# A routed-expert kernel: four weight loads moved later, filler matmuls on TensorE, and two of four result tables read and added while the last experts run

## What is computed

```
x = x + attention(norm(x))      # 16 heads, 4 kv heads, causal, soft cap, rotary
x = x + ffn(norm(x))            # routed experts + shared expert
x = x + recurrence(norm(x))     # h = a*h + u over the 2048 tokens
x = x + ffn(norm(x))            # the same ffn weights again
# ffn: softmax of x @ gate.T over 64 experts, best 3 of 8 groups, best 6 experts of them
slot = flat * 96 + min(pos, 95)                 # 96 rows per expert
buf[slot] = x[tok]                              # (64*96, 256)
out = (silu(buf @ Wg.T) * (buf @ Wu.T)) @ Wd.T  # M = 176
y = sum over the 6 choices of out[slot] * weight;  return y + shared(x)
```

## Time and profile before

| what | us |
|---|---|
| median of 3 runs (lowest, highest) | 1233.53 (1233.43, 1235.91) |
| the profiled execution, its own time | 1236.23 |
| its span, first to last instruction | 1234.1 |
| TensorE busy | 997.5 |
| DVE busy | 520.1 |
| ACT busy | 739.3 |
| POOL busy | 410.5 |

### The profile page before, as it was taken

One profiled execution on the slowest core, in us unless ns is written; L12 is line 12 of the kernel. 1 busy time (PEld: TensorE's weight loads), 2 busy tenths in 40 slices (PEclk: granted clock), 3 DMA queues, 4 the chain that ended last, 5 costly groups with the idle time before them and its releaser, 6 DMA issues.

```text
span 1234.1 us, 20310 instructions
## 1 busy us (share of the span) xinstructions
PE 997.5 (81%) x7268; PEld 644.7 (52%) x7268; DVE 520.1 (42%) x1575; ACT 739.3 (60%) x982; POOL 410.5 (33%) x404
## 2 busy tenths in 40 slices
...
GB/s 352 394 392 78 1 1 1 18 2 11 49 50 23 18 33 90 2 21 4 142 264 234 292 289 290 109 151 271 50 121 109 160 66 125 268 290 279 268 63 330
DMA packets 94948, 176.21 MB, mean 143 GB/s; under 512 B 13134, under 2 KB 46895, under 8 KB 94848
## 3 DMA queue, kind: packets, MB, share of 16 engines
...
## 4 chain that ended last, share of the span: by engine, by line
PE 29%; POOL 11%; issue 4%; DMA 3%; DVE 3%; DVEq 1%; ACT 0%; POOLq 0%; SPq 0%; ACTq 0%
PE PS L1459 14%; PE PS L1470 9%; POOL expert_in L335 8%; POOL pause L343 3%; PE PS L1446 2%; PE PS L1515 1%; DMA XE<-expert_in 1%; PE PS L1499 1%; DMA spare_space<-expert_out 1%; DMA expert_in<-xp,didx 1%; PE PS L1548 1%; DMA expert_out<-ob,yidx 1%; PE PS L1389 0%; PE PS L1404 0%; POOL expert_out L1345 0%
## 5 line engine op out<-in xcount | busy, mean ns | idle before, releaser
L335 POOL DMA_INDIRECT expert_in<-xp,didx x192 | 193.6, 1008 | 618.2 <-ACT PR L779 496.6
L774 ACT ACTIVATE PR<-PS 128x1024 f32<-128x1024 f32 (+3 forms) x312 | 276.5, 960 | 30.8 <-PE PS L643 15.2
L779 ACT ACTIVATE PR<-PR 128x2048 f32<-128x2048 f32 (+3 forms) x156 | 274.1, 1759 | 0.0
L1345 POOL DMA_INDIRECT expert_out<-ob,yidx x128 | 180.6, 1411 | 157.4 <-ACT ob L1657 117.5
L663 PE MATMUL PS<-PR,V 128*32 128x512 f32 (+3 forms) x768 | 94.9, 568 | 43.4 <-ACT PR L779 43.4
L1906 DVE SCALAR_TENSOR_TENSOR gta<-gth,PS 88x192 f32<-88x192 f32 x128 | 44.8, 350 | 192.8 <-ACT gth L1647 192.8
L643 PE MATMUL PS<-QT,KT 96*128 96x512 bf16 (+3 forms) x384 | 103.7, 363 | 12.4 <-ACT PR L774 9.8
L1647 ACT ACTIVATE gth<-PS 88x192 f32<-88x192 f32 x128 | 41.8, 326 | 106.6 <-PE PS L1459 106.6
L1657 ACT ACTIVATE ob<-PS,wslot 96x256 f32<-96x256 f32 x128 | 60.1, 469 | 62.1 <-PE PS L1470 59.9
L1459 PEld LDWEIGHTS PS<-XT,spare_space 128*88 128x88 f32 x960 | 91.7, 163 | 8.8 <-issue 2.6
L668 PE MATMUL PS<-PR,V 128*32 128x256 f32 x960 | 66.8, 392 | 34.9 <-ACT PR L779 34.6
...
## 6 DMA issues: line engine op xcount, KB each, us to landing
...
spare_space<-expert_out SPq DMA_DIRECT2D x24, 512.0 KB, 6.2
...
```

The source lines that it names most:

```text
L335: pool.indirect_dma_start(out=buf_d[f], out_offset=bass.IndirectOffsetOnAxis(ap=didx[b][:, r, j:j + 1], axis=0), in_=xp[b][:, r, :], in_of ...
L774: act.activation(PR[:, n % 3, 2 * pr:2 * pr + 2, cols(v, s):CW], PS[:, S0 + 2 * pr:S0 + 2 * pr + 2, cols(v, s):CW], ACT.Tanh, scale=1.0 / ...
L779: act.activation(PR[:, n % 3, :, lo:CW], PR[:, n % 3, :, lo:CW], ACT.Exp, scale=SOFT_CAP).then_inc(exp_done, 1)
L1345: pool.indirect_dma_start(out=y_d[f], out_offset=bass.IndirectOffsetOnAxis(ap=yidx[:, n % 4, j:j + 1], axis=0), in_=ob[:, i % EU, :], in_o ...
```

## The change

It has five parts. Line numbers in it differ from those of the profile before.

1. **Late fetch (f = 0 only).** SP waits until the first `XE` load has landed before it issues the weights of places 10 to 13, and `wab` after them.
2. **Fillers.** `fill(n)` on TensorE issues n matmuls of the identity with 256 columns into a bank whose content nobody reads: 14 ahead of either `experts`, 12, 4 and 13 around the first overflow matmuls, 12, 8, 8 and then 2 at a time in the recurrence loop, 15 ahead of the last combination.
3. **Tables.** `table_of` gives experts 0 to 43 four tables as before, 44 to 55 three (0, 1, 2), and 56 to 63 two (0, 1). A send waits for the last send to the same table, which is now 4, then 3, then 2 experts back.
4. **Retired tables.** Table 3 is complete after expert 43, table 2 after expert 55. `retired_tables` on SP reads each in four pieces (chunks, 512 KB in runs of 1 KB) into `TA` and `TB`, which take the place of ring places whose experts are done; DVE adds the pieces of table 3 to X after experts 50, 52, 54 and 56, and those of table 2 after expert 63.
5. **At the end two tables are read** (`LATE = 2`), 2 KB per partition and tile in place of 4 KB, with one add less on DVE or two matmuls less on TensorE for each tile. `add_results(2)` moves behind `recur_inputs(0)`.

```diff
+LATE = 2
+TABLE_GROUPS = (0, 11, 12, 13, 14)
+def table_of(e):
+    return e % 4 if e < 44 else (e - 44) % 3 if e < 56 else e % 2
+def last_in_table(e, j):
+    return max([i for i in range(e) if table_of(i) == j], default=None)
...
+        TA, TB = (place_at(NACC * i, NACC).rearrange("p (i n) -> p i n", i=NT) for i in range(2))
+        GB = place_at(0, LATE).rearrange("p (r n) -> p r n", r=CT)
...
+            def retired_tables(f):
+                for j, space, used in ((3, TA, (46, 48, 50, 52)), (2, TB, (58, 59, 60, 61))):
+                    last = f * E + last_in_table(E, j)
+                    sp.wait_ge(y_sent[last % EU], 16 * (last // EU + 1))
+                    if j == 2:
+                        sp.wait_ge(tables_added, (2 * f + 1) * NC)
+                    for c in range(NC):
+                        sp.wait_ge(down_psum, f * E + used[c])
+                        rows = y_d[f][NACC * CW * c:NACC * CW * (c + 1), :]
+                        sp.dma_start(space[:, CT * c:CT * (c + 1), :], rows.rearrange("(i p k) c -> p i k c", p=P, k=NACC)[:, :, j, :])\
+                          .then_inc(table_ld[c], 16)
...
             first_spare(0)
+            sp.wait_ge(x_ld[0], 16)
+            first_spare2(0)
             sp.dma_start(wab[:], wab_d).then_inc(wab_loaded, 16)
-            first_spare2(0)
             experts(0)
+            retired_tables(0)
...
-                if e >= NACC:
-                    pool.wait_ge(y_sent[(i - NACC) % EU], 16 * ((i - NACC) // EU + 1))
+                if last_in_table(e, table_of(e)) is not None:
+                    last = f * E + last_in_table(e, table_of(e))
+                    pool.wait_ge(y_sent[last % EU], 16 * (last // EU + 1))
...
+            def fill(n, bank=V0):
+                for _ in range(n):
+                    pe.matmul(PS[:, bank, 0:2 * P], const("ident"), consts[:, 0:2 * P], start=True, stop=True, skip_group_check=True)
...
+                pe.wait_ge(out_copied, 2 * E)
+                fill(15)
                 pe.wait_ge(o95_loaded, 32)
-                pe.wait_ge(out_copied, 2 * E)
...
+            fill(14)
             experts(0)
+            pe.wait_ge(out_copied, E)
+            fill(12)
             overflow_rows(0)
+            fill(4)
             overflow_rows(1)
+            fill(13)
             turn_recur(0)
             for c in range(NC + 1):
                 k = NC + c - 1
                 if c:
+                    fill(8 if c == 1 else 2)
                     turn_rows(k)
                     logits(k)
                 if c < NC:
                     gates(c)
+                if c == 0:
+                    fill(12)
...
                 if c < NC:
+                    fill(8 if c == 0 else 2)
                     turn_state(c)
...
+            def add_table(f, j, space, c):
+                dve.wait_ge(table_ld[c], 16 * (2 * f + j + 1))
+                xc = X[:, CT * c:CT * (c + 1), :]
+                dve.tensor_tensor(xc, xc, space[:, CT * c:CT * (c + 1), :], ALU.add).then_inc(tables_added, 1)
...
+                    if e in (50, 52, 54, 56):
+                        add_table(f, 0, TA, (e - 50) // 2)
+                for c in range(NC):
+                    add_table(f, 1, TB, c)
...
-            add_results(2)
             for c in range(NC + 1):
...
                 if c < NC:
                     recur_inputs(c)
+                if c == 0:
+                    add_results(2)
```

41 lines of the change are left out of this document (19 added, 22 removed).

## The result

The changed kernel takes **1262.49 us** (median of 4 runs, 1255.8 to 1266.1); the kernel before, run beside it, 1234.72 us (median of 4, 1233.43 to 1236.26). The ratio is 1.0222 with a 95% interval of 1.0187 to 1.0256: slower by 28 us. I had said 1229.0 and 1211 to 1240, so both the number and the direction were wrong. The profiled execution of the changed kernel took 1264.41 us, its span is 1262.6.

What follows compares the result with a forecast made beforehand. TensorE was taken to bound the expert stages, transfers and a relay of engines the joints between. Terms -6.0 + 19 + 3 - 8.5 - 12 = -4.5 us gave 1231.7 profiled, 1229.0 us on the median's scale; range 1211 to 1240.

Steps and rivals of the forecast that it cites:

- The reads of table 3: Both expert stages: DVE waits behind expert 50 for a piece queued behind weights, then the clock is low; +19 us.
- Sends closer together: Last experts of both stages: sends on fewer tables wait for landings, delaying the last send; +3 us, bounds 0 and 15.
- two tables pace the last experts: Rival, from expert 56: landings at 6.6 us pace the sends, 15 us in place of 3, total 1241; chance 0.18.
- The end: After the last send: fewer bytes read and TensorE kept fast by 15 fillers; -12 us, bounds -5 and -13.
- the fillers do not hold the clock: Rival, at the end: the clock drops before O95 lands, giving 5 us in place of 12, total 1236; chance 0.12.
- Reading back in f = 0: Between the stages: fewer adds and bytes, and fillers, bring POOL's first dispatch earlier; -8.5 us, bounds -5 and -11.
- Late fetch: Start of the f = 0 experts: holding weights and wab back lets the first input land sooner; -6.0 us.
- Fillers ahead of the experts: Start of both stages: 14 fillers end 5 and 7 us before the inputs, so stages start at 1.2 GHz; nothing.
- The pieces of table 3 are in time: Rival, behind expert 50: the pieces arrive without a DVE wait, the 19 us fall away, total 1210; chance 0.17.

Runs made afterwards that it cites:

- experiment 3: Kernel before with only the change's tables and send waits (four, three, then two), all four tables read at the end, no late fetch or fillers: 1236.12 us.
- experiment 8: experiment 1 with only table 3 retired, three tables used and read to the end, 22 fillers behind the last expert: 1226.88 us.
- experiment 9: experiment 6 with DVE's adds of table 2 held until every send has landed and O95 read first: 1228.14 us.
- experiment 6: experiment 1 with 32 fillers in place of 15 behind the last expert: 1232.1 us.
- experiment 4: Kernel before with the late fetch and all fillers of the change, its four tables left as they were: 1231.26 us.
- experiment 7: experiment 1 without the 12 fillers ahead of chunk 2's overflow matmuls and with 17 in place of 8 ahead of the first transposes of rows: 1236.55 us.
- experiment 12: Kernel retiring table 3 alone, with the middle's fillers as in experiment 7, and 34 and 43 in place of 14 fillers ahead of the experts: 1223.34 us.
- experiment 1: Changed kernel with DVE adding table 3's pieces behind experts 56 to 59 in place of 50, 52, 54 and 56, reads unmoved: 1241.52 us.

## Why the prediction was wrong

Sum predicted: -4.5 us. Sum measured: +28.5. All five terms missed to the slow side: the end by 11.2 us, the reads of table 3 by 9.0, the sends by 6.0, reading back by 3.6 (dispatch included) and the late fetch by 2.9. The end alone would have brought the forecast to 1240, table 3 alone to 1238, the edge of the range. The misses were not independent of each other: the waits of the tables also spoilt the fillers of the end. By its own steps:

- **The reads of table 3** (+19, measured +28.0) are the largest cost, as large as the whole loss. The mechanism, the place and the clock's 3 us were right. The bytes were right for f = 0 (2.0 MB, measured 2.12) and too few for f = 1 (1.85, measured 2.49). What failed is the sentence "Sends and input loads dry up once DVE stands, so I let the queue run at 290 GB/s". They went on holding 40% of the engines, and the queue ran at 177 GB/s. My 2.0 MB at 177 GB/s are 11.3 us, and the wait in f = 0 was 11.0; the 1.85 MB of f = 1 would be 10.5 us, and the 13.8 measured there need the larger 2.49 MB as well. The upper bound of 14 us a stage, "if it does not speed up at all", was the truth, and I had not asked what speed it had: the earlier trace rows give 1.44 MB in 15 us and 0.85 MB in 10.5, 96 and 81 GB/s with the engines partly idle, and nothing in them says 290. That is the rate of a queue nearly alone: from 634 to 640 of the kernel before SP's queue moved 1.69 MB, 282 GB/s, with 94% of the engines.
- **Sends closer together** (+3, measured +9.0). I put the landing beside the reads of table 2 at 5.5 us and spread it evenly. Experiments 3, 8 and 9 show it otherwise: the pace alone costs 2 us for both stages, the reads of table 2 on top of this pace the rest, through one wait of 3.6 to 3.7 us at the moment when the engines are full, and a string of sends behind it that only closes up by tenths. My rival *two tables pace the last experts* had this mechanism and priced it at 15 us. It was true by half, and it was not alone.
- **POOL beside DVE's adds** was missing from the sum ("nothing" for the four adds of table 2). POOL's issue took 1.71 to 2.43 us while they ran, 1.41 without. The Trainium skill ("SBUF — State Buffer", SBUF: two separate sides) says that a DVE instruction with two SBUF inputs and a GpSimd instruction that reads SBUF lock each other out of a shared pair of ports; by that rule the trace agrees. It was hardly on the path: without it the lags fell by 0.7 and 1.7 us (experiment 9 against 6).
- **The end** (-12, measured -0.8). The working was right: experiment 6 brings the end to 22.1 us. What failed is "kept busy by 15 fillers until O95 is there". That holds with a lag of 5 us, as experiment 4 shows, and the step before had already moved `O95` away from it by 3 us in my own sum, in fact by 5.3. The fillers ended 5.2 us early and the clock was lost for the whole end. The rival *the fillers do not hold the clock* gave 5 us for it, and was right about the outcome but not the reason: fillers held the clock through 14 us in experiment 6. From the Trainium skill ("TensorE: Matmul & The Clock Gate", Part 1) I had put at most 12 us on all fillers together. Experiments 6 and 7 gained 10.8 and 3.9 us at their joints, 14.7 in all, of which up to 2.7 are not the clock's but the wait for the misplaced overflow matmuls: 12.0 to 14.7 us, at or a little above the bound that I had worked out from the Trainium skill.
- **Reading back in f = 0** (-8.5, measured -3.6, with another -1.3 in the dispatch). Again the working is borne out, by the 8.7 us of experiment 7, and the fillers' places are not. I had seen the 12 fillers ahead of chunk 2's overflow, but expected them by 843 with DVE waiting till then, and took the 8 ahead of `turn_rows` to reach it. They ended 3.6 us short.
- **Late fetch** (-6.0, measured -3.1, and -3.3 alone). From 640 to 648 SP's queue still moved bytes beside the input:

```profile
q10 hardware_dynamic: 800, 1.00, 62.8%
q1 hardware_dynamic: 202, 0.41, 18.8%
```

  TensorE started 7.3 us behind the issue of the load at 640.0, not 4.4. I had compared it with a load of f = 1 beside which nothing was in flight, and had taken the 2.59 MB of the earlier trace rows for "just that amount" of the four pairs and wab, where in the changed kernel, with those held back, 0.41 MB of weights issued ahead of them still move here. By the Trainium skill ("DMA: Bandwidth & Descriptors", Queues, rings and completion order) I had worked out a gain of 2 to 3 us, and set it aside for the shares of a window of 16 us, longer than the load itself. In the kernel before SP's and ACT's queues held 72.7% and 32.7% of the engines from 642 to 644, and 49.5% and 46.6% from 644 to 646, so the trace agrees with equal turns only in the second of these. That the gain of 2 to 3 us came out is luck as far as the runs show: it rested on a load of 6 or 7 us in the kernel before, where TensorE started 10.5 us behind the issue.
- **Fillers ahead of the experts** (nothing) came out as nothing: they ended 9.0 and 10.1 us before the inputs, not 5 and 7, both stages began at 1.2 GHz, and experiment 12 shows that longer ones shorten the stages by 1.6 and 3.0 us and the whole by nothing, through the sends in f = 0 and through a start 2.4 us later in f = 1.
- *The pieces of table 3 are in time* was the rival whose place experiment 1 shows: with the adds six experts later the change costs 6 us in place of 28, and with fitted fillers (experiment 6) it is 3 us under the kernel before.

Taken together: two of the gains were there to be had and were lost by fillers whose number did not fit. At the end the fit was spoilt by the waits that the other half of the change had put ahead of it, since with four tables the same 15 fillers reach (experiment 4). In the middle the fillers stood in the wrong places whatever the tables.
